# A two-layer transformer with routed experts on one core: four expert tiles moved earlier, and Silu written as tanh and products on GpSimd

## The reference, cut to what matters

```python
xn = layernorm(x)
x = x + attention0(xn) + fp4_ffn(xn)      # fp4_ffn: h = silu(gate) * up, width 352, inputs quantized in blocks of 16
xn = layernorm(x)
x = x + attention1(xn) + moe(xn)

def moe(xf):
    logits = relu(xf @ Wr1 + br1) @ Wr2 + br2
    tg, ti = top_k(softmax(logits), 2);  tg = softmax(tg / 2)
    out = silu(xf @ Ws1 + bs1) @ Ws2 + bs2                 # shared expert, width 512
    for e in range(8):                                     # routed experts, width 512
        h = silu(xf @ We1[e] + be1[e]) @ We2[e] + be2[e]
        out = out + sum(tg * (ti == e)) * h
    return out
```

## Time and profile before

| what | value |
|---|---|
| time, median of 3 runs | 1354.55 us (1351.75 to 1355.31) |
| the profiled execution | 1353.15 us, its span 1351.4 us |
| PE matmul busy | 1099.4 us, 81% of the span |
| DVE busy | 931.3 us, 69% |
| ACT busy | 791.7 us, 59% |
| POOL busy | 458.6 us, 34% |
| mean granted TensorE clock | 0.957 |

### The profile page before, as it was taken

The page is one execution under the profiler, slowest core; times in us unless marked ns, Lnnn a source line. Parts: engine busy times, 40 slices in busy tenths (PEclk is TensorE's granted clock), DMA queues, the critical chain, the costliest instruction groups (busy, mean ns, idle before and its releaser), DMA issues.

```text
span 1351.4 us, 19322 instructions
## 1 busy us (share of the span) xinstructions
PE 1099.4 (81%) x6711; PEld 496.0 (37%) x6711; DVE 931.3 (69%) x1599; ACT 791.7 (59%) x1063; POOL 458.6 (34%) x410
## 2 busy tenths in 40 slices
PE   2578688888988888889888988898888658888885
PEld 1213323323432343234323432342233246777741
DVE  6878577888878886878787868777864336732233
ACT  1255475667686767675767675767676513233364
POOL 8641362242333233223323332321241212334320
PEclk9879788999999999999999999999999879999987
DMA  5622065117312721372136305620611356555553
GB/s 142 147 64 63 9 185 147 36 38 194 111 36 77 193 72 37 102 188 57 32 118 178 80 2 143 170 57 1 165 32 45 107 171 164 186 165 187 167 168 108
DMA packets 149632, 146.73 MB, mean 109 GB/s; under 512 B 13696, under 2 KB 142016, under 8 KB 149536
## 3 DMA queue, kind: packets, MB, share of 16 engines
q1 hardware_dynamic: 144048, 135.58, 36.6%
q0 software_dynamic: 4544, 9.38, 2.1%
q10 hardware_dynamic: 944, 0.54, 0.1%
HBM read 92.80 MB, written 52.12 MB: 107 GB/s over the span
## 4 chain that ended last, share of the span: by engine, by line
PE 35%; DVE 19%; ACT 16%; issue 7%; DMA 7%; DVEq 6%; SPq 5%; POOL 2%; ACTq 0%; POOLq 0%
DVE nm L1043 11%; PE sums L388 8%; ACT ex L761 8%; PE mx L400 7%; PE mx L369 4%; ACT L737 4%; PE mx L494 3%; PE mx L485 3%; PE ring L290 2%; DMA qs<-xsort 2%; PE ring L469 2%; DMA ks<-xsort 2%; PE ring L300 2%; DVEq L993 1%; PE ring L295 1%
## 5 line engine op out<-in xcount | busy, mean ns | idle before, releaser
L1043 DVE TENSOR_REDUCE nm<-mx 128x2 f32<-128x1024 f32 x512 | 600.9, 1216 | 112.4 <-PE mx L369 111.0
L761 ACT ACTIVATE ex<-mx 128x1024 f32<-128x1024 f32 x512 | 511.3, 1024 | 272.4 <-PE mx L400 272.1
L400 PE MATMUL mx<-qs,ks 128*128 128x512 bf16 (+1 forms) x1024 | 298.5, 390 | 39.6 <-ACT ex L761 11.0
L388 PE MATMUL sums<-ex,vs 128*18 128x512 f32 x2048 | 283.4, 613 | 4.3 <-ACT ex L761 1.7
L369 PE MATMUL mx<-km,qm 32*128 32x512 bf16 x1024 | 149.1, 397 | 77.7 <-DVE nm L1043 37.3
L400 PEld LDWEIGHTS mx<-qs,ks 128*128 128x128 bf16 (+1 forms) x1024 | 76.4, 99 | 316.8 <-ACT ex L761 124.7
L1484 POOL TENSOR_SCALAR binade<-binade 128x704 f32<-128x704 f32 (+1 forms) x24 | 56.9, 2370 | 247.5 <-DVE binade L994 247.5
L369 PEld LDWEIGHTS mx<-km,qm 32*128 32x128 bf16 x1024 | 38.3, 91 | 229.1 <-issue 76.5
L1509 POOL DMA_INDIRECT xsort<-xn,pos_i x64 | 62.6, 977 | 103.1 <-DVE pos_i L1124 85.8
L1476 POOL TENSOR_TENSOR parts<-qk_f,parts 128x512 bf16<-128x512 f32 x32 | 37.6, 1196 | 149.5 <-DVE parts L962 149.5
L1447 POOL TENSOR_TENSOR rstd<-veps,minus_half 128x4 f32<-128x4 f32 x16 | 16.7, 1045 | 183.6 <-DVE veps L953 183.6
(11 more groups left out here) (216 smaller groups left out, 1502.2 us busy)
## 6 DMA issues: line engine op xcount, KB each, us to landing
scratch<-parts SPq DMA_DIRECT2D x128, 256.0 KB, 3.6
ks<-scratch SPq DMA_DIRECT2D x64, 256.0 KB
qs<-scratch SPq DMA_DIRECT2D x64, 256.0 KB
qs<-wmoe SPq DMA_DIRECT2D x20, 578.0 KB, 3.8
ks<-wmoe SPq DMA_DIRECT2D x19, 578.0 KB, 3.8
qm<-scratch SPq DMA_DIRECT2D x64, 128.0 KB, 2.6
km<-scratch SPq DMA_DIRECT2D x64, 128.0 KB, 2.6
rest<-parts SPq DMA_DIRECT2D x32, 128.0 KB
```

Source lines behind the costliest of these rows:

```text
L388: done = pe.matmul(acc[32 * j:32 * j + 2 * VW, :], values[:, start:start + 2 * VW], ex[:, s % NEX, j, :], start=q == 0 and t == 0, stop=q ...
L400: done = pe.matmul(bank[:, j, :], ks[l][r, h, t * P:(t + 1) * P], qs[l][r, h, :], start=True, stop=True)
L761: act.activation(ex[:, s % NEX, 2 * i:2 * i + 2, :], bank[:, :, :], ACT.Exp, scale=SCALE).then_inc(free, 1)
L1043: dve.tensor_reduce(nm[l][:, t, h:h + 2], bank[:, :, :], AX.X, ALU.max, negate=True).then_inc(free, 1)
```

## The change

**Silu.** `gates` and `shared_hidden` write silu(x) = x/2 + x/2 * tanh(x/2). ACT makes two passes over the bank: tanh into a scratch tile, and x/2 into h_sb or hs, and frees the bank after the second. GpSimd then multiplies (scratch = scratch * h) and adds (h = h + scratch). The load_table calls of the turns go away. The scratch is a part of the tile `work`, which all calls share (the prologue's gates use two parts of ex, the last batch's shared_hidden uses qk_f). A counter, `silu_set`, numbers the calls: ACT waits before its tanh until the call before is done on GpSimd; DVE's ffn_up and PE's shared_out wait for their own call.

**Tail.** Tile steps 0 to 3 stand in turn_b(7) behind slots 9, 11, 13 and 15, each with a Silu and an Exp table load on ACT. turn_a(8) and on runs tile_step(4 + k), the maxima of the last attention run in every other step (k = 2, 4, ..., 32), its max_rows at k = 20 and behind the last step. SP fetches weights 0 to 3 and tokens 0 to 3 ahead of the last stores, tile 4 between load_max and store_late, and from there on tokens before weights.

```diff
-FIRST_TILE = 0
+TILE_SLOTS = (9, 11, 13, 15)
+AHEAD = len(TILE_SLOTS)
+SHARED_TILES = (AHEAD + 6, AHEAD + 7)
...
+        def gate_use(b, i):
+            return 4 * b - 2 + i if b else i
+        def hidden_use(b, i):
+            return (4 * b + 4 if b < LAST else 4 * b + 2) + i
+        def gate_tanh(b, i):
+            a = work[:, 0:2 * F0].rearrange("p (t f) -> p t f", f=F0) if b else ex[:, 1, 2 * i:2 * i + 2, 0:F0]
+            return a
+        def hidden_tanh(b):
+            return work[:, 0:2 * T].rearrange("p (c t) -> p c t", t=T) if b < LAST else qk_f[:, :, :]
...
         def units_a(b, k):
+            if b == B:
+                return [(1, LAST, (k - 2) // 2)] if k % 2 == 0 and 2 <= k < 2 + 2 * SLOTS else []
...
             def shared_out(b):
-                pair_read(pe, ("H", b, 1))
+                pe.wait_ge(silu_set, hidden_use(b, 1) + 1)
...
+                    if b == LAST and k in TILE_SLOTS:
+                        tile_step(TILE_SLOTS.index(k))
...
+            for k in range(SLOTS, NTILE + 1 - AHEAD):
+                if k == 20:
+                    max_rows(1, LAST, 0)
+                for unit in units_a(B, k):
+                    for i in range(2):
+                        maxima(*unit, i)
+                tile_step(AHEAD + k)
+            max_rows(1, LAST, 1)
...
+            def gates(b, i):
+                bank, free = from_pair(("gate", b, i))
+                wait(act, silu_set, gate_use(b, i))
+                act.activation(gate_tanh(b, i), bank[:, :, 0:F0], ACT.Tanh, scale=0.5)
+                act.activation(h_sb[:, 2 * i:2 * i + 2, :], bank[:, :, 0:F0], ACT.Identity, scale=0.5).then_inc(free, 1)
+            def shared_hidden(b, i):
+                bank, free = from_pair(("H", b, i))
+                act.wait_ge(halved, 1)
+                act.wait_ge(silu_set, hidden_use(b, i))
+                if b == LAST:
+                    act.wait_ge(p3_ready, 2 * B)
+                for j in range(2):
+                    c = 2 * i + j
+                    act.activation(hidden_tanh(b)[:, j, :], bank[:, j, :], ACT.Tanh, bias=b1_half[:, c:c + 1], scale=0.5)
+                    done = act.activation(hs[:, c, :], bank[:, j, :], ACT.Identity, bias=b1_half[:, c:c + 1], scale=0.5)
+                done.then_inc(free, 1)
-            def gates(b, i):
-                if b >= 1:
-                    load_table(ACT.Silu, 8 * b + 2 * i)
-                bank, free = from_pair(("gate", b, i))
-                act.activation(h_sb[:, 2 * i:2 * i + 2, :], bank[:, :, 0:F0], ACT.Silu).then_inc(free, 1)
-                if b >= 1:
-                    load_table(ACT.Exp, 8 * b + 2 * i + 1)
...
+                    if b == LAST and k in TILE_SLOTS:
+                        load_table(ACT.Silu, 8 * B + 2 * TILE_SLOTS.index(k))
+                        tile_hidden(TILE_SLOTS.index(k))
+                        load_table(ACT.Exp, 8 * B + 2 * TILE_SLOTS.index(k) + 1)
...
             def ffn_up(b, i):
-                pair_read(dve, ("gate", b, i))
+                dve.wait_ge(silu_set, gate_use(b, i) + 1)
...
+            def silu(h, t, n):
+                pool.tensor_tensor(t, t, h, ALU.mult).then_inc(silu_half, 1)
+                pool.wait_ge(silu_half, n + 1)
+                pool.tensor_tensor(h, h, t, ALU.add).then_inc(silu_set, 1)
...
             round_weights(2)
+            for i in range(2):
+                gates(0, i)
             third_part(0, 1)
...
                 if b >= 1:
+                    for i in range(2):
+                        shared_hidden(b - 1, i)
                     scatter(b - 1)
                 if b + 1 <= LAST:
                     round_x(b + 1)
                 normalize(1, b)
                 residual1(b)
+                if b + 1 <= LAST:
+                    for i in range(2):
+                        gates(b + 1, i)
                 if b + 2 <= LAST:
                     normalize(0, b + 2)
...
             for i in range(NTILE):
+                if i in SHARED_TILES:
+                    shared_hidden(LAST, SHARED_TILES.index(i))
                 scatter_results(i)
...
                     fetch_tokens(0)
-                    fetch_weights(1)
                     fetch_tokens(1)
+                    for i in range(1, NW):
+                        fetch_weights(i)
+                    for i in range(2, AHEAD):
+                        fetch_tokens(i)
                 store_early(1, b)
                 load_max(1, b)
+                if b == LAST:
+                    fetch_tokens(AHEAD)
+                    fetch_weights(AHEAD)
                 store_late(1, b)
...
-                fetch_weights(i)
                 fetch_tokens(i)
+                fetch_weights(i)
+            load_rows(1, LAST, 1)
```

More of the change, by code:

```diff
@@ L154, in two_layers @@
         hs = sb("hs", [P, EC, T])
+        b1_half = sb("b1_half", [P, EC])
         r1_sb = sb("r1_sb", [32, T])
@@ L541, in work_a @@
                         shared_hidden(b - 1, 1)
-                    if at == (11 if b == 1 else 9, "a"):
+                    if b < B and at == (11 if b == 1 else 9, "a"):
                         max_rows(1, b - 1, 0)
@@ L875, in turn_a @@
                     work_a(b, k, "d")
-                    if b > LAST and k >= FIRST_TILE:
-                        tile_hidden(k - FIRST_TILE)
+                    if b > LAST:
+                        tile_hidden(AHEAD + k)
             def turn_b(b):
@@ L915, in _ @@
             turn_a(B)
[L916 to L919, removed]
+            for k in range(SLOTS, NTILE + 1 - AHEAD):
+                if k == 20:
+                    max_rows(1, LAST, 0)
+                if AHEAD + k < NTILE:
+                    tile_hidden(AHEAD + k)
+            max_rows(1, LAST, 1)
             for k in range(SLOTS):
@@ L1359, in turn_a @@
                     work_a(b, k, "c")
-                    if b > LAST and k >= FIRST_TILE:
-                        tile_step(k - FIRST_TILE)
+                    if b > LAST:
+                        tile_step(AHEAD + k)
             def turn_b(b):
@@ L1503, in round_weights, with gates, shared_hidden @@
                 round_and_scale(w, w.shape[1], fp4_binade(n), qsc[1 + n], fp4_done, n + 1 if n else 0)
+            def silu(h, t, n):
+                pool.tensor_tensor(t, t, h, ALU.mult).then_inc(silu_half, 1)
+                pool.wait_ge(silu_half, n + 1)
+                pool.tensor_tensor(h, h, t, ALU.add).then_inc(silu_set, 1)
+            def gates(b, i):
+                pair_read(pool, ("gate", b, i))
+                h = h_sb[:, 2 * i:2 * i + 2, :]
+                silu(h, gate_tanh(b, i), gate_use(b, i))
+            def shared_hidden(b, i):
+                pair_read(pool, ("H", b, i))
+                h = hs[:, 2 * i:2 * i + 2, :]
+                silu(h, hidden_tanh(b), hidden_use(b, i))
             def scatter(b):
@@ L1746, in _ @@
                 load_stacks(1, b, 0)
-            for i in range(2, NTILE):
-                if i == 4:
+            for i in range(AHEAD + 1, NTILE):
+                if i == AHEAD + 4:
                     sp.wait_ge(ends_ready, 1)
```

23 lines of the change are left out of this document (8 added, 15 removed).

## The result

The changed kernel takes 1422.22 us (1415.09 to 1424.28, four runs) against 1354.93 us for the kernel before in the same comparison: ratio 1.0491, interval 1.0450 to 1.0532. It is slower by 67.3 us, as forecast in sign, but by more than twice the forecast 29.5 us, and outside the range. The profiled execution took 1424.28 us, its span 1422.5 us, at a mean granted clock of 0.910 instead of 0.957.

The account below looks back on a forecast made before the run. It took a chain of waits, owned by no engine (PE 35% of the span), to bound the kernel. Profiled 1353.15 us + 38 (ACT's stalls in the turns) + 10 (clock) - 17 (tail) = 1384 us, range 1355 to 1404.

Parts of the forecast that it names:

- The products alone would be off the path: In the turns, GpSimd's products by themselves cost nothing; only ACT's wait for the shared scratch does.
- Turn_a(2) to (7): Shared expert's second call: ACT waits for GpSimd's products, +1.8 us a turn, 10.8 for six.
- Prologue: 0 +- 1.5: gates(0,*) have their own scratch; an extra pass each and one load fewer before the first Exp: 0 +- 1.5 us.
- The stall in turn_b: Second gate call: ACT stands 5.3 us for GpSimd's products; slot 8's exponential +3.05 us, 18.3 for six turns.
- the point of decision: In turn_b of batch 5, GpSimd's products done by 793.1 would break even; the sum had them end at 796.1.
- rival A: Products end before ACT wants the scratch: turn_b gains 2.3 us, turn_a 1.1; 1312 us in all; chance 9%.
- Turn_b(0) and turn_a(1): The same stalls in these two turns: +5.0 us in turn_b(0), +4.4 in turn_a(1).
- The clock: After each turn_b stall PE runs at the lower clock, losing up to 1.6 us: 6 x 1.6 = +10 us.
- The tail: From turn_b(7) on: moved tiles -2 us, removed token waits -18, 2.7 given back; -17 in all (0 to -21).
- The products' length: GpSimd's two-input products in the turns: 1.68 us at 704 columns, 2.37 us at 1024.
- D: Rival: the tail gains nothing and every stall in the turns costs clock, 1410 us; chance 8%.
- E: Rival: Tanh reloads tables, two loads per call back in the turns, +36 us, 1420 us; chance 2%.

Follow-up runs that it names:

- e7: e4 with the shared expert's products cut into pieces of 256 columns: 1330.20 us, ratio 0.9806.
- e9: The changed kernel, one scratch and all waits kept, with only the shared expert's products in pieces of 256 columns: 1410.46 us, ratio 1.0422.
- e4: e3 with a second scratch, so that ACT waits for the call before last: 1362.64 us, ratio 1.0055.
- e5: The kernel before with four unread GpSimd products of 128x1024 in every turn_a from the first batch's on: 1376.48 us, ratio 1.0133.
- e6: e5 with its unread products cut into sixteen pieces of 256 columns: 1355.87 us, ratio 0.9996.
- e3: The changed kernel without ACT's scratch wait in the prologue's gates(0, 1): 1414.13 us, ratio 1.0430.
- e8: New tail; tanh and GpSimd products with two scratches only for gates of batches 2 to 7, Silu with loads elsewhere: 1321.92 us, ratio 0.9737.
- e1: The changed kernel with gates and shared expert as before, so the new tail alone: 1335.05 us, ratio 0.9861.
- e2: The changed kernel with the old tail, so the Silu part alone: 1439.76 us, ratio 1.0627.

## Why the prediction was wrong

- **"The products alone would be off the path"** is the step that failed: it put what the products do to VectorE at nothing. Off every semaphore's path, they still held VectorE's short instructions to their end, and behind the hold PE stood and its clock fell. Turn_a(2) to (7) came to +31.9 us where 10.8 was forecast, which is 21 of the 40 us that the sum missed (prologue 7.4, tail 6.1, the rest smaller). Four kernels split these six turns, each against before: hardly any wait or hold (e7) -4.1, ACT's wait alone (e9) +17.9, the hold alone (e4) +24.8, both +31.9. The two do not add up simply, since VectorE's hold partly falls into the time in which ACT stands anyway. That it is the hold, and not GpSimd's time, e5 and e6 show in the kernel before (+15.2 and -2.1 in these turns). The Trainium skill's SBUF — State Buffer (SBUF: two separate sides) states this: GpSimd and VectorE share a pair of ports, as an exclusive lock for the whole instruction, against VectorE operations in a two-port mode or with two SBUF inputs. The rows agree: casts, copies and two-input instructions on SBUF are held to within 0.06 us of the product's end, a reduction takes its usual 0.17 us. It was the rule that spoke against this change, and the prediction did not weigh it. So two engines hold each other up here where no semaphore stands, which the description of the core, with engines that meet only at semaphores, leaves out.
- **The sign was there.** The kernel before has the hold already, where the earlier trace rows show two products of GpSimd from 199.04 on, 1.16 us each. The same cast and two-input instruction, 0.18 and 0.17 us long in turn_a(6), stand there so:

```profile
199.59 0.65 DVE L1085 CAST lidxf<-lidx 128x32 f32<-128x32 uint32 x1
...
200.65 0.68 DVE L1103 TENSOR_TENSOR gpair<-le,gsum 128x8 f32<-128x8 f32 x1
```

- **"Prologue: 0 +- 1.5"** failed by an oversight, +7.4: I saw that the scratch was separate and did not see that ACT waits all the same, with q and k behind it. e3 shows it.
- **The stall in turn_b** was right: 5.34 us for 5.3, slot 8 late by 3.45 for 3.05, and with the clock 4.9 a turn for 4.65. e4 and e8 show the point of decision from the other side: with the stall away, each turn gains 2.07, as rival A had it.
- **Turn_b(0) and turn_a(1)** came to +7.2 and +6.3 for +5.0 and +4.4; these carry a share of hold and clock that the runs do not separate.
- **The clock** was about right as a term of turn_b (0.7 to 2.1 us for 1.6), but turn_a was given none, and its granted clock fell to 0.91 to 0.93 (0.98 to 1.00 before). e9 shows the fall behind the wait alone, e4 behind the hold alone, and e7, with hardly any of either, has the clock of before. What part of turn_a's 5.3 us is clock the runs do not separate.
- **The tail**, -17 forecast, was -19.1 alone (e1), though not by the terms as I split them, so that the near total is partly luck. Tile 5 entered 4.8 us later than forecast (86.4 us into turn_b(7)), for the larger part since the split came 11 us later, not 8; but the kernel before itself reached tile 5 only 93.3 us into the turn, for I had run its tiles 3 and 4 without waits. Moving the tiles thus brought 6.9 us instead of 2, and what follows tile 5 brought 12.7 instead of 15.3. With the Silu part the same tail is worth less (-10.9), and e2 shows +7.8 there for Silu alone. Most of that arises at the two slots of the last batch's shared expert (in e2 tile 8 enters 0.8 us later than before, tile 10 already 5.6 us); why was not settled.
- The products' length was right: 1.67 us for 704 columns and 2.36 for 1024, as the rows had it; the Trainium skill's figure (GPSIMD Engine Reference, 3.1) gave 1.55 and 2.25 as estimates and was 5 to 7% low.
- Of the rivals, none is what happened. D's 1410 us is nearest, but its first reason, a tail that gains nothing, is refuted by e1; its second, that every stall costs clock, turn_a bears out. E (tables reloaded) is excluded: no load stands before a tanh in the turns, or in turn_a(8), where Tanh runs under Silu's table.

## What to carry to other kernels

Before work is moved to GpSimd, list what VectorE does in that stretch: every cast, copy and two-input instruction on SBUF may wait there for the whole of a running GpSimd instruction, so keep GpSimd's instructions short (here 256 columns; sixteen in a row took 9.55 us of GpSimd in e6) or put them where VectorE reads PSUM (two reductions of the maxima, which do, kept their 2.34 us under e4's products). A shared scratch makes the second of two calls as slow as the queue of the engine that empties it; look at what stands ahead there, and give a call its own scratch before anything else is judged. A change of several parts should be measured in parts: this one, 4.9% slower, held a tail worth 1.4% and a turn worth another 0.9%.

## What was not expected of the hardware

Cutting GpSimd's products from 1024 to 256 columns removed the whole cost, as far as can be measured, rather than three quarters of it (e6: ratio 0.9996, 0.9974 to 1.0018, with a cast and a two-input instruction still taking 0.50 and 0.46 us instead of 0.18 and 0.16). The reduction behind them still had to wait 0.29 us for PE: what is left fits, it seems, into VectorE's idle time. And a hold of some 2 us on an instruction of 32 columns shows in the trace as that instruction's own length (2.25 us against 0.18), with no wait beside it: only the comparison with the same line elsewhere tells it, in the other kernel or, as turn_a(1) had it, in another turn of the same one.
